# An attention and expert kernel with its set-up, its handover and its end reordered

## The reference, cut to what matters

```python
q = einsum('bsh,oh->bso', normed, q_w)          # normed = rms(layernorm(x)) * norm_w
k = einsum('bth,oh->bto', concat([normed, ctx]), k_w)
attn = softmax(where(mask, q @ k.T * scale, -inf))
alpha = sigmoid(layernorm(x) @ gate_w.T + gate_b)
x = x + (1 - alpha) * layernorm(x) + alpha * (attn @ concat([normed, ctx]))
h = gelu(gathered @ W1[e] + b1[e]);  out_e = h @ W2[e] + b2[e]
x = x + scatter_add(out_e * combine_weights)    # gathered = layernorm(x)[top_idx]
```

## Time and profile before

| | |
|---|---|
| median of 3 runs | 276.33 us (275.99 to 277.49) |
| profiled execution, its own time | 277.63 us |
| span of its profile | 275.8 us |
| mean granted TensorE clock | 0.991 |
| PE busy | 265.7 us (96%) |
| DVE busy | 219.0 us (79%) |
| ACT busy | 188.2 us (68%) |
| POOL busy | 155.9 us (57%) |

### The profile page before, as it was taken

How to read it: one execution, slowest core, us unless ns; L and a number is a source line. 1 busy time by engine, 2 the same in 40 slices (tenths; PEclk the granted TensorE clock), 3 DMA queues, 4 the chain that set the end, 5 groups by cost and what they waited for, 6 DMA issues and landing times.

```text
span 275.8 us, 5127 instructions
## 1 busy us (share of the span) xinstructions
PE 265.7 (96%) x1474; PEld 226.7 (82%) x1474; DVE 219.0 (79%) x554; ACT 188.2 (68%) x349; POOL 155.9 (57%) x153
## 2 busy tenths in 40 slices
PE   6999999999989999999999999999999999999992
PEld 2688899999866888888888888888888888888992
DVE  1788999898986499968878896796887889689452
ACT  2488898887575976685677587658657758763540
POOL 4283865655843956556446466655645646605515
PEclk9799999999999999999999999999999999999998
DMA  7993247568454956455565544546555461201211
GB/s 219 358 263 94 77 123 218 155 214 276 114 182 123 350 160 157 124 192 167 138 195 163 154 139 135 157 122 209 156 138 189 156 175 53 67 26 47 62 38 69
DMA packets 30292, 42.44 MB, mean 154 GB/s; under 512 B 5251, under 2 KB 24015, under 8 KB 30148
## 3 DMA queue, kind: packets, MB, share of 16 engines
q1 hardware_dynamic: 25392, 30.00, 34.4%
q0 software_dynamic: 4608, 12.24, 15.4%
q10 hardware_dynamic: 276, 0.00, 0.1%
HBM read 33.54 MB, written 9.24 MB: 155 GB/s over the span
## 4 chain that ended last, share of the span: by engine, by line
PE 83%; DVE 6%; issue 4%; POOL 3%; ACT 2%; DMA 1%; DVEq 0%; POOLq 0%; ACTq 0%
PE bank L1398 19%; PE bank L1185 13%; PE bank L1186 12%; PE bank L1187 12%; PE bank L1399 10%; PE bank L1229 4%; PE bank L1274 3%; PE bank L1326 2%; PE bank L1345 1%; PE bank L1349 1%; PE bank L1346 1%; DMA x_all<-in_x_dram 1%; PE bank L1181 1%; POOL out_dram L552 1%; PE bank L1258 1%
## 5 line engine op out<-in xcount | busy, mean ns | idle before, releaser
L742 ACT ACTIVATE keysT<-bank,biasT 128x512 f32<-128x512 f32 x63 | 43.7, 693 | 55.6 <-PE bank L1187 41.8
L552 POOL DMA_INDIRECT out_dram<-h,sidx x32 | 36.8, 1151 | 41.9 <-DVE h L1077 37.0
L543 POOL DMA_INDIRECT x_all<-out_dram,idx_all x32 | 35.4, 1106 | 23.9 <-DMA out_dram<-h,sidx 16.5
L1185 PE MATMUL bank<-x_hi,w_parts 128*128 128x512 f32 (+1 forms) x114 | 45.1, 396 | 0.0
L1186 PE MATMUL bank<-x_lo,w_parts 128*128 128x512 f32 (+1 forms) x114 | 44.4, 389 | 0.0
L1187 PE MATMUL bank<-x_hi,w_parts 128*128 128x512 f32 (+1 forms) x114 | 44.1, 387 | 0.0
L1102 DVE TENSOR_TENSOR g_lo<-keysT,g_hi 128x512 fp32r<-128x512 f32 x32 | 22.1, 690 | 24.9 <-ACT g_hi L743 23.4
L1398 PE MATMUL bank<-w_parts,g_hi 128*128 128x512 f32 x112 | 40.5, 396 | 0.0
L539 POOL DMA_INDIRECT x_all<-token_rows,idx_all x28 | 29.0, 1036 | 19.4 <-DVE factor L1126 7.7
L1107 DVE TENSOR_TENSOR w_parts<-w_raw,w_parts 128x512 fp32r<-128x512 f32 x56 | 38.9, 696 | 0.0
L748 ACT CAST w_parts<-w_raw 128x512 fp32r<-128x512 f32 x56 | 34.9, 623 | 0.0
(11 more groups left out here) (186 smaller groups left out, 685.9 us busy)
## 6 DMA issues: line engine op xcount, KB each, us to landing
w_raw<-in_L_ffn_W_dram SPq DMA_DIRECT2D x32, 512.0 KB
idx_rows<-in_L_ffn_top_idx_dram SPq DMA_DIRECT2D x8, 256.0 KB, 4.0
out_dram<-x SPq DMA_DIRECT2D x8, 256.0 KB, 3.0
hn_cnat<-in_ctx_dram SPq DMA_DIRECT2D x7, 256.0 KB, 2.7
token_rows<-xn SPq DMA_DIRECT2D x7, 256.0 KB, 2.2
hn_cnat<-in_L_ffn_b_dram SPq DMA_DIRECT2D x1, 1024.0 KB, 6.9
x_all<-in_x_dram SPq DMA_DIRECT2D x3, 256.0 KB, 4.4
x_all<-in_x_dram SPq DMA_DIRECT2D x1, 768.0 KB, 8.1
```

The lines of the kernel that those rows point to most:

```text
L543: g.indirect_dma_start(accg[:, t, :], None, flat, list_of(e, t)).then_inc(acc_in[t], 16)
L552: g.indirect_dma_start(flat, idx(sidx[:, t:t + 1].bitcast(U32), 0), newrow[:, t, :], None, bounds_check=N - 1, oob_is_err=False).then_inc( ...
L742: a.activation(g32[:, f % NG, :], ps_up[f % 2][:, :], ACT.Gelu_apprx_tanh, bias=bias)
L1185: t_.matmul(dst, lhs_hi, rhs_hi, start=first, stop=False)
```

## The change

1. Set-up loads: k_w goes to ACT's queue, ahead of norm_w; gate_b is loaded by partition beside it, and the two rows are no longer loaded. On SP's queue the first context comes third. Ten `junk` products in place of nine.
2. Set-up products: both halves of M come first, then the rows' transposes, the context's transposes, and four transposes that spread norm_w and gate_b in place of the product with ones. The first query waits for the high part of the rows alone; the passes with the low part come last in each half.
3. Set-up on ACT and DVE: `M_high(1)` ahead of `hn_transposed`, the context's copy ahead of `normed_transposed`; `M_low(1)` ahead of `hnT_low`; the statistics of sequences 6 to 9 are split and partly moved into `attention(0)`.
4. Chunks 2 and 3 of expert 0's weights are issued after the third context.
5. Handover: POOL issues tiles 0 to 2 of the first gathers after `x_plus_h` of the last pair and tile 3 after `rstd`; the high part of `late_rows(0)` moves behind the transposes of the probabilities; the order of the remaining products is changed and the last rows' parts interleaved; the last list load goes behind the last rows' stores.
6. `seen` is filled as 1,024 words in place of 2,048 half words, and with its four selects comes ahead of expert 1's gathers.
7. End: in the last expert `down` of block 4 is moved into `last_downs`, so `up` of blocks 6 and 7 follow each other; `take_waits` is left out before the last scatters.

```diff
             load_x(0, 0, 2)
             load_weight(0, q_w, wts_in)
-            load_weight(1, k_w, wts_in)
+            load_ctx(0)
             load_x(1, 2, 4)
-            load_ctx(0)
...
-            for c in range(NCH):
-                sp.dma_start(w_chunk_dst(c), w_chunk(0, c)).then_inc(w_in[c], 16)
+            for c in range(2):
+                load_chunk(0, c)
...
             load_ctx(2)
+            for c in range(2, NCH):
+                load_chunk(0, c)
...
                         sp.dma_start(rows_v[:, 2 * r + b, 0:H], xn_last[:, b, :]).then_inc(xn_out[r % 2], 16)
+                    sp.wait_ge(onehot_rdy, NB - EARLY)
+                    load_lists(IDX_PARTS - 1)
...
-                    sp.wait_ge(onehot_rdy, NB - EARLY)
-                    load_lists(IDX_PARTS - 1)
...
-                    gather_first_rows(range(1, NT))
+                    gather_first_rows(range(NT - 1))
...
-                if p == LAST - 1:
-                    gather_first_rows(range(1))
+                if is_last(p):
+                    gather_first_rows(range(NT - 1, NT))
...
-                    take_waits(pool)
+                    if not is_last(e):
+                        take_waits(pool)
...
+            pool.wait_ge(pv_mm, NPAIR)
+            pool.wait_ge(last_xn[1], 1)
+            g.memset(seen_pairs, ONE_ONE).then_inc(consts, 1)
+            pool.wait_ge(consts, 4)
+            for t in range(NT):
+                g.affine_select(out=seen[:, t, :], in_=seen[:, t, :], compare_op=ALU.is_ge, fill=DUP, base=-t,
+                                pattern=[[1, C]], channel_multiplier=-NT).then_inc(seen_rdy, 1)
...
             gather_rows(1, 1)
-            pool.wait_ge(pv_mm, NPAIR)
-            g.memset(seen, 1.0).then_inc(consts, 1)
...
+            act.dma_start(wts[:, 1, :, :], k_w.rearrange("(k p) h -> p k h", p=P)).then_inc(wts_in, 16)
...
             M_high(0)
+            M_high(1)
             hn_transposed(0, 0)
-            M_high(1)
+            context_transposed(0, 0)
...
             query(0)
-            context_transposed(0, 0)
...
             hn_rows(0, 0)
-            x_sums(2, 3, 1)
             dve.wait_ge(nwT_in, 16)
             M_low(0)
-            x_sums(3, 4, 1)
+            M_low(1)
             hnT_low(0, 0)
+            x_sums(2, 4, 1)
             x_aggregates(2, 4)
-            M_low(1)
...
-            x_stats(6, 10, 3)
-            x_variances(6, 10)
+            x_sums(6, 8, 3)
...
+                    x_sums(8, 10, 3)
                     hnT_low(1, 1)
...
                 if is_first(p):
+                    x_aggregates(6, 10)
+                    x_variances(6, 10)
...
+            last_pair_low(0)
             last_pair_shift(1)
...
+            last_pair_low(1)
...
             M_rows(0)
+            M_rows(1)
             hn_transposes(0, 0)
-            M_rows(1)
-            pe.wait_ge(vec_in, 32)
-            pe.wait_ge(ones_rdy, 1)
-            t_.matmul(banks[7][:, :], ones_row[:, :], vec_rows[:, :], start=True, stop=True).then_inc(bc_mm, 1)
+            context_transposes(0, 0, 0)
+            pe.wait_ge(nwT_in, 16)
+            pe.wait_ge(gate_b_in, 16)
+            for n in range(2):
+                for k in range(KH):
+                    last = t_.transpose(banks[7][:, (n * KH + k) * P:(n * KH + k + 1) * P],
+                                        norm_w_gate_bT[:, n, k:k + 1].broadcast_to([P, P]), ident[:, :])
+            last.then_inc(bc_mm, 1)
             pe.wait_ge(setup_lo, 2)
-            query(0, 0)
-            context_transposes(0, 0, 0)
+            pe.wait_ge(hnT_hi_rdy, 1)
+            for m in range(KH):
+                c = slice(m * P, (m + 1) * P)
+                for k in range(KH):
+                    t_.matmul(ps_q[:, m, :], M_hi[:, k, c], hnT_hi[:, 0, k, :], start=(k == 0), stop=False)
+                    t_.matmul(ps_q[:, m, :], M_lo[:, k, c], hnT_hi[:, 0, k, :], start=False, stop=False)
+                pe.wait_ge(hnT_lo_rdy, 1)
+                for k in range(KH):
+                    last = t_.matmul(ps_q[:, m, :], M_hi[:, k, c], hnT_lo[:, 0, k, :], start=False, stop=(k == KH - 1))
...
                 if is_last(p):
-                    early_rows(range(1))
+                    pe.wait_ge(log_rdy, 2 * NPAIR - 1)
+                    pe.wait_ge(late_hi_rdy, 1)
+                    for b in range(2):
+                        late_rows(0, b, late_hi, first=b == 0)
...
+            early_rows(range(1))
+            pe.wait_ge(late_lo_rdy, 1)
             for b in range(2):
-                pe.wait_ge(late_hi_rdy, 3 + b)
-                late_rows(2, b, late_hi)
+                late_rows(0, b, late_lo)
+            early_rows(range(1, NT - 1))
+            pe.wait_ge(late_hi_rdy, 2)
+            for b in range(2):
+                late_rows(1, b, late_hi)
+            early_rows(range(NT - 1, NT))
+            pe.wait_ge(late_hi_rdy, 3)
+            late_rows(2, 0, late_hi)
+            pe.wait_ge(late_lo_rdy, 2)
+            for b in range(2):
+                late_rows(1, b, late_lo)
             for k in range(KH):
+                cols = slice(k * P, (k + 1) * P)
+                pe.wait_ge(late_hi_rdy, 4)
+                t_.matmul(ps_xT[k][:, :], late_hi[2][:, 1, cols], onehot[:, 5, :], start=False, stop=False)
...
-                    for f in range(NF - 3, NF):
+                    for f in range(NF - 4, NF):
...
-                    if not (is_last(e) and f == NF - 1):
+                    if not (is_last(e) and f >= NF - 2):
                         down(e, s, f - 2)
```

More of the change, by code:

```diff
@@ L51, in build_xattn_moe @@
     MASKED = -1e30
+    ONE_ONE = 1.0 + 0x3F80 / 2 ** 23
     LAST = 7
@@ L147, in build_xattn_moe @@
             .rearrange("p (t c) -> p t c", t=NT)
+        seen_pairs = normed[:, :, :, :].rearrange("p s b h -> p (s b h)")
         cnat_last = x_all[:, NT * ROW:NT * ROW + 2 * H].rearrange("p (b h) -> p b h", b=2)
@@ L558, in _ @@
             gather_rows(1, 1)
-            pool.wait_ge(pv_mm, NPAIR)
-            g.memset(seen, 1.0).then_inc(consts, 1)
-            pool.wait_ge(consts, 4)
-            for t in range(NT):
-                g.affine_select(out=seen[:, t, :], in_=seen[:, t, :], compare_op=ALU.is_ge, fill=DUP, base=-t,
-                                pattern=[[1, C]], channel_multiplier=-NT).then_inc(seen_rdy, 1)
             def expert(e, s):
@@ L585, in _ @@
             a = nc.scalar
-            act.dma_start(norm_wT[:, :], norm_w.rearrange("(k p) -> p k", p=P), allow_slow_non_contiguous=True)\
+            act.dma_start(wts[:, 1, :, :], k_w.rearrange("(k p) h -> p k h", p=P)).then_inc(wts_in, 16)
+            act.dma_start(norm_wT, norm_w.rearrange("(k p) -> p k", p=P), allow_slow_non_contiguous=True)\
                 .then_inc(nwT_in, 16)
-            act.dma_start(vec_rows[:, 0:H], norm_w.rearrange("(a h) -> a h", a=1)).then_inc(vec_in, 16)
-            act.dma_start(vec_rows[:, H:2 * H], gate_b.rearrange("(a h) -> a h", a=1)).then_inc(vec_in, 16)
+            act.dma_start(norm_w_gate_bT[:, 1, :], gate_b.rearrange("(k p) -> p k", p=P),
+                          allow_slow_non_contiguous=True).then_inc(gate_b_in, 16)
             for s in range(2):
@@ L674, in attention @@
                     normed_transposed(2, 0)
-                    for c in range(NCH):
+                    for c in range(2):
+                        act.wait_ge(w_in[c], 16)
+                elif not isinstance(p, int) and s == 0:
+                    for c in range(2, NCH):
                         act.wait_ge(w_in[c], 16)
@@ L1030, in _ @@
                             ALU.mult, ALU.add).then_inc(last_xn[1], 1)
-            for b in range(2):
-                dve.wait_ge(late_hi_rdy, 3 + b)
-                dve.wait_ge(last_xn[b], 1)
-                v.tensor_tensor(late_lo[2][:, b, :], xn_last[:, b, :], late_hi[2][:, b, :].bitcast(F32),
-                                ALU.subtract).then_inc(late_lo_rdy, 1)
+            last_pair_low(1)
             def x_lo_part(e, s):
@@ L1162, in _ @@
             pe.wait_ge(warm_rdy, 1)
-            keep_warm(9)
+            keep_warm(10)
             pe.wait_ge(wts_in, 32)
@@ L1250, in attention @@
                         .then_inc(setup_mm, 1)
-                    pe.wait_ge(log_rdy, 2 * NPAIR - 1)
-                    pe.wait_ge(late_hi_rdy, 1)
-                    for b in range(2):
-                        late_rows(0, b, late_hi, first=b == 0)
                 pe.wait_ge(exp_rdy, 2 * p + 2)
@@ L1301, in _ @@
             each_pair(pe, attention)
-            early_rows(range(1, NT))
-            for n in range(2):
-                if n:
-                    pe.wait_ge(late_hi_rdy, n + 1)
-                    for b in range(2):
-                        late_rows(n, b, late_hi)
-                pe.wait_ge(late_lo_rdy, n + 1)
-                for b in range(2):
-                    late_rows(n, b, late_lo)
-            for b in range(2):
-                pe.wait_ge(late_hi_rdy, 3 + b)
```

(11 more changed lines are left out.)

26 lines of the change are left out of this document (16 added, 10 removed).

## The result

The changed kernel takes 274.98 us (median of 7 runs, 274.6 to 275.13). The kernel before took 277.49 beside it (7 runs, 275.99 to 280.45); the ratio is 0.9935, with a 95% interval of 0.9913 to 0.9956 (it leaves out the run of 280.45, which is in a slower state, and is not the quotient of the two medians). Forecast were 272.8 us and a range of 271.2 to 274.9. It is faster, as forecast, but by less, and the time lies just above the range.

The account below looks back on a forecast made before the run. PE was taken as the bound (busy 96%, 83% of the chain), leaving start, handover and end to gain. 1.3 + 1.2 + 1.0 = 3.5 us took the median from 276.33 to 272.8 us, range 271.2 to 274.9.

Parts of the forecast that it names:

- the start's 1.3 us: Start to first pairs: first logits 2.3 to 2.7 us earlier, of which 1.3 us arrive; bounds 0.3 and 2.3.
- The two pieces that leave PE's path: Start: M's second half between transposes and query (1.71 us) and the product with ones (1.45 us) leave PE's path.
- the whole 3.5: Whole kernel: summed gain of start, handover and end, 3.5 us, taking the median from 276.33 to 272.8 us.
- the count of POOL's list: First pairs: POOL's `x_plus_h` of pair 1 ends at 28.0 instead of 29.3 us; residual's stall stays, 1.3 us arrive.
- The rival that the start gives nothing: Start: late x, gate_b's load or POOL's longer list takes its gain; 274.1 us, chance 0.18.
- x's price: Start: x's first load comes later because k_w loads beside it; 0 to 0.8 us, taken as 0.5.
- The handover, forecast 1.2 (0.8 and 0.4): About 71 to 87 us: 0.8 from `x_plus_h` ahead of the gather, 0.4 from PE's new order; bounds 0.3 and 1.6.
- their rows are there near 94.5, needed near 96: Handover: expert 1's gathers start near 86.6 us, so their rows arrive before PE needs them.
- a transfer takes the handover's place: Handover: rival; late last list or expert 1's rows make ACT or PE wait 1.5 us or more; 274.3 us, chance 0.10.
- The end, forecast 1.0: After the last products: POOL's four scatters start 1.1 us earlier and no longer queue; 1.0 us, bounds 0.5 and 1.3.
- the wait at 266.87 goes, 0.1 to 0.2 us: End: block 7's earlier `up` puts its gelu and `g_lo` under block 4's products, removing PE's wait, 0.1 to 0.2 us.
- the rival of a slower time: Start: PE's gaps bring the lower clock from 8 to near 20 us, costing 5.3 us; 278.1 us, chance 0.04.

Follow-up runs that it names:

- end_only: The kernel before with only the end's edits (part 7 of the change); 275.55 us, ratio 0.9977.
- the lower group: Of 103 runs of the kernel before, the 63 between 275.84 and 276.55 us; middle 276.15 us.
- start_only: The kernel before with only the set-up's edits (parts 1 to 4 of the change); 276.33 us, ratio 0.9994.
- handover_only: The kernel before with only the handover's edits (parts 5 and 6 of the change); 276.34 us, ratio 0.9984.
- stats_back: The changed kernel with the statistics of x for sequences 6 to 9 back ahead of the mask, in one piece; 275.27 us.
- kw_on_sp: The changed kernel with k_w loaded from SyncE's queue behind q_w instead of from ScalarE's; 276.10 us.
- sum_low: sum_early with tile 0's half of the low part put ahead of the early rows' first tile on TensorE; 274.31 us.
- before_warm: The kernel before with one more junk product ahead of M and three between M's first half and the first transposes; 276.29 us, ratio 0.9987.
- sum_early: pool_order with the second `x_plus_h` ahead of the powers of 10 to 15 on GpSimd; 274.06 us, ratio 0.9903.
- pool_order: The changed kernel with the powers and shifts of sequences 6 to 9 on GpSimd moved behind the first `x_plus_h` and second normed rows; 274.77 us.
- seen_back: The changed kernel with the preparation of `seen` back behind expert 1's gathers on GpSimd, in its old form; 274.82 us.
- best2: sum_early with tile 0's low part earlier on TensorE and the last expert's first add_bias later on VectorE; 274.22 us.

## Why the prediction was off

**The sum was made against an execution whose excess was one of its own terms.** The prediction says that the profiled execution "lies 1.3 us above the median of the runs, so the median goes from 276.33 to 272.8". The excess was not neutral: it is the lower clock from 7.8 to 11.2 us, and the start's 1.3 us were the removal of just this. The two pieces that leave PE's path were priced from the same rows, 1.71 and 1.45 us at the lower clock; from the start of M's second half to the first query it is 3.29 us in the profiled execution and 2.11 in end_only, at a clock of 1.00. Against the profiled execution the forecast was 274.1 and the time 275.13, 1.0 off; carrying the whole 3.5 over to the median counted 1.3 twice. Of the 2.2 us by which 272.8 was missed this is the larger part. Beside the lower group the parts came to 0.0, 0.7 and 0.65: 276.15 less 1.35 is 274.8, and the two sets of runs gave 274.98 and 274.69.

**The start, forecast 1.3.** Its marks held: first logits at 12.24 (12.1 to 12.5 forecast), and 1.13 of the 1.3 us arrived beside the profiled execution. But with equal clock it is 0.0. The step that failed is the count of POOL's list as the only holder: it gives the residual's stall (which stayed, 1.72, as forecast), and not that DVE's own queue is all but full from 10 us on (0.66 us idle up to the residual in start_only) and does the same work behind earlier logits, 18.5 us in place of 17.2 from the first to pair 2's. The rival that the start gives nothing was right in size for the lower group, by DVE and not by x. x's price was forecast at 0.5 and is 0.12. On the rule of the Trainium skill (DMA: Bandwidth & Descriptors, "Issuing engines are not separate DMA queues") the runs agree with what it says, that a second queue saves only issue time: M starts 0.4 us earlier in the mean for an issue 1.0 earlier. What I drew from it, that x would be late by its full share of 0.8, they don't show. The small load of gate_b and the later chunks were hidden.

**The handover, forecast 1.2 (0.8 and 0.4).** The mechanism was right and so was the size up to `up`: 1.13 to 1.16 in the two executions with the least wait for tile 0. `mix` took 0.77 (0.7 forecast). The step that failed is "their rows are there near 94.5, needed near 96": they are there at 94.8 to 95.0, and needed from 94.4 on. 0.53 to 0.75 us arrive in the three profiles of handover_only and the changed kernel. Here the rival "a transfer takes the handover's place" had the kind, late gathered rows: expert 1's cost 0.3 to 0.6 us in two executions, and the wait for tile 0's (0 to 1.63 us), which the new place of the gather causes, stands nowhere in the prediction; it counted tile 3's.

**The end, forecast 1.0.** 0.68. Queueing on POOL gave the forecast 1.00. What was wrong is "the wait at 266.87 goes, 0.1 to 0.2 us": it goes, and waits of 0.10 and 0.27 us for the low parts of blocks 6 and 7 come before it.

**The clock** didn't fall in the changed kernel; the rival of a slower time has nothing for it. **From 32 us on** PE carried what it was given, as forecast.

## What to carry to other kernels

Ask first of which kind the profiled execution is: if its time lies well above the median, find what in it is long (here the granted clock in one-microsecond windows), and don't subtract that once more from the median. An earlier result on one engine is worth only what the engine that consumes it can take up; follow the fullest queue behind it to where TensorE becomes full, and count its work as conserved. And where DVE's instruction takes twice its usual time, look for POOL's beside it before looking at the order of anything else: two moves on POOL, the powers and one `x_plus_h`, gave 0.6 us, as much as the whole last stage of the change.

## What the hardware showed that I hadn't expected

The time of a whole kernel can fall into two groups, 1.4 us apart, one run in three in the upper, and in the upper one that was profiled TensorE's granted clock was down for 3.4 us at the start. Kernels with a group of runs above their others are the kernel before, end_only (4 of 12), stats_back (3 of 12), kw_on_sp (5 of 12), sum_low (1 of 12). Their profiles have TensorE's longest idle stretches between 5 and 17 us, 0.96 to 2.01 us, while before_warm, start_only and the changed kernel, with 0.57 to 0.63, have no such runs. But sum_early, with 0.97, has none in six, and every profiled execution except the one was granted 1.00 there. So the idle time of one execution doesn't tell which group another falls into. handover_only, pool_order, seen_back and best2 spread over 1.4 to 2.2 us, for which no profile gives the cause. Small instructions of DVE, on six numbers per partition, take up to 1.0 us longer beside POOL's 128x512 addition or multiplication (0.85 for 0.16, 1.21 for 0.17), as much as the big ones do.
